# The mixing stage of a two-layer convolution kernel: steps of 8 rows instead of 4, and another split of the nine depthwise taps

## The chip, the cores and the metric

The kernel runs on one core of a Trainium2 chip, in one launch. The metric is the device time of that launch in microseconds (us). The kernel before takes 5684.54 us in the median of three runs (5683.73 to 5684.84). Engines: PE is TensorE (matmuls), PEld its weight loads, DVE VectorE, ACT ScalarE, POOL GpSimd, SP SyncE, which here only issues DMAs.

## The reference

The input `x` is (8, 128, 256, 256) in float32. Two layers follow each other. In short:

```python
# layer 0
h = concat(haar_dwt(group_norm(x)))            # 4*128 channels, 128x128 pixels
h = gelu(batchnorm(conv1x1(h, w_c1, b_c1)))    # 128 channels
res = h
o = dwconv3x3(h, dw_w, dw_b)                   # nine taps per channel, zero padding
o = layernorm_chw(o, gn_g, gn_b)               # mean and variance over one batch element
o = gelu(conv1x1(o, pw1_w, pw1_b))
h = conv1x1(o, pw2_w, pw2_b) + res             # called u in the kernel
h = gelu(batchnorm(conv1x1(h, w_c2, b_c2)))    # 4*128 channels
x = x + haar_idwt(h)
# layer 1
x = x + blur4x4(group_norm(x))
```

## The kernel before, in words

The work is in three stages, one after the other, each a block of instruction streams, one stream an engine. `phase_conv1` (lines 157 to 404) reads `x`, works out its statistics and writes `z`, the output of the first 1x1 convolution without its batch norm, to a scratch in HBM (`z_scratch`), with sums for the batch norm beside it. `phase_mix` (lines 439 to 850) is the mixing stage: batch norm and gelu of `z`, depthwise convolution, layer norm, two pointwise convolutions, residual. It writes `u` to `u_scratch`, and adds up the Gram matrix of `u` (128x128, and the sums as column 129), from which the batch norm of the third stage is worked out. `phase_tail` does the rest. The change touches `phase_mix` alone and the constants ahead of it.

In the mixing stage the 128 channels lie on the partitions. A unit of work is 4 rows of 128 pixels, 512 columns wide, one PSUM bank; a batch element has `STEPS` = 32 units, all eight have `ALL2` = 256. The loops are unrolled in Python: each engine has a loop over a step number `p`, and in each step it does different parts for different units. What a unit `e` goes through:

- SP loads its 4 rows of `z` into `z_in` (L545, four slots).
- ACT does gelu with the batch norm's scale and shift into `h_ring`, called `plane` in the code (L810). It holds 41 blocks of 4 rows with a zero column at each side; between two batch elements lies a block of zero rows, set by POOL (L582). `plane` keeps `h` until the residual reads it.
- The nine taps of the depthwise convolution are split. PE does 2 (`PE_TAPS`) as matmuls with diagonal matrices into `dw_psum`, which has two banks used in turn (L730). DVE does 4 as multiply-adds on `dw_psum`, in place, the fourth into `depthwise_out` (L650); each waits for the one before. ACT does 3 as products with a scale into `tap_products` (L838). POOL adds the three products in two adds (L601) and then adds their sum to `depthwise_out` (L605).
- DVE takes statistics of the finished unit (L657, `bn_stats`).
- After the last unit of a batch element DVE, PE and POOL work out mean and variance over all channels (L665 to L677, L780, L593 with `pow`), and DVE folds the result into the weights and bias of the first pointwise convolution (L682 to L684, L689, with L783 on PE).
- The second half of a unit `l` runs `LEAVE` = 39 steps behind `p`, 35 or 36 behind its depthwise work, since it needs the statistics of its whole batch element: pointwise matmul 1 (L746), gelu (L820), pointwise matmul 2 (L739), residual on DVE (L638), store of `u` (L550), four transposes into `transpose_psum` (L755), copy to SBUF by ACT (L827), four Gram matmuls (L765).

So there are three stretches: 36 steps with depthwise work alone (the filling), 220 with both halves, and 36 to 37 with the second half alone (the draining). The order of the parts inside a step is written out by hand in each engine's loop (L698, L769, L841, L586, L552). Every float32 matmul appears as two records in the trace, and as one half of a `x2` in the rows here.

Of the kernel before, what the change touches and what calls it, by code (L numbers as in the profile page):

```python
# [19 lines left out]
BANK = 512  # L20
# [407 lines left out]
LAG_Z = 1  # L428
LAG_TR = 1
LAG_EVAC = 2  # L430
LAG_GRAM = 3
LAG_DW = 3
LAG_TAPS = 4
LAG_LAST = 3
LAG_STATS = 5
AHEAD = 2


def phase_mix(nc, kp, pw1, pw2, const, z_d, u_d):
# [3 lines left out]
    with ExitStack() as ctx:  # L443
# [3 lines left out]
        plane = sb("h_ring", [128, 4 * BLOCKS + 2, W2 + 2])  # L447
        o_buf = sb("depthwise_out", [128, O_SLOTS, BANK])
        z_in = sb("z_in", [128, 4, BANK])
        diag = sb("tap_diagonals", [128, PE_TAPS, C])  # L450
# [3 lines left out]
        v_t = sb("gelu1_out", [128, 2, BANK])  # L454
        products = sb("tap_products", [128, 2, ACT_TAPS, BANK])
        u_t = sb("u_tile", [128, 4, BANK])
        u_tr = sb("u_transposed", [128, 2, 4, C + 1])
        bst = sb("o_stats", [128, STEPS, BN_W])
# [11 lines left out]
        small = ps("small2", [128, 4])  # L470
# [11 lines left out]
        s_z = [sem(f"z_loaded{i}") for i in range(4)]  # L482
        s_h = sem("h_rows_ready")
        s_dw = sem("dw_psum_ready")
# [15 lines left out]
        s_gm = sem("gram_step_done")  # L500
        s_gacc = sem("gram_added")
        s_ust = [sem(f"u_stored{i}") for i in range(4)]
# [5 lines left out]
        def block_of(e):  # L508

            return e // STEPS * (STEPS + 1) + e % STEPS  # L510

        def tap(k, e):

            kh, kw = k // 3, k % 3
            r = block_of(e) % BLOCKS * R2 + kh
            return plane[:, r:r + R2, kw:kw + W2]

        def rows_of(e):
            r = 1 + block_of(e) % BLOCKS * R2
            return plane[:, r:r + R2, 1:1 + W2]  # L520

        def freed_by(at):

            if at < BLOCKS:
                return None
            b, j = divmod(at - BLOCKS, STEPS + 1)
            return b * STEPS + min(j, STEPS - 1)
# [8 lines left out]

        @block.sync
        def _(sp):
            sp.dma_start(K[:, 0:C], const[:, 0:C]).then_inc(s_id, 16)

            def load(e):
                if e >= 4:
                    sp.wait_ge(s_h, e - 3)
# [948 lines left out]
```

## Time and profile before

| | |
|---|---|
| median of three runs | 5684.54 us |
| the profiled execution's own time | 5687.8 us |
| span of its instructions | 5685.9 us |
| first stage | 0 to about 1237 us |
| mixing stage | about 1237 to 2583 us |
| third stage | about 2583 us to the end |
| busy over the whole span: PE, DVE, ACT, POOL | 92%, 77%, 65%, 36% |
| mean granted clock of TensorE | 0.968 |
| DMA rate in the mixing stage, steps with both halves | 102 to 111 GB/s |

The page of the profile cuts the span into 40 equal slices of 142 us. Of these the mixing stage holds the slices 9 to 18. In them POOL, which does nothing in the first stage, is 7 to 8 tenths busy, DVE 9, ACT 7 to 8, and PE 9, which in the page stands for 90% or more. A busy share says how much of an engine's time is taken and not what holds a step up; for that the rows below come from the timeline.

### The profile page before, as it was taken

What the parts mean: (1) busy time and instruction counts of PE and PEld (TensorE: products, weight loads), DVE (VectorE), ACT (ScalarE), POOL (GpSimd) and SP (SyncE); (2) the same over time, 40 slices, a digit from 0 to 9 for tenths busy, and PEclk for the clock granted to TensorE, in tenths of its full rate; (3) what the DMA queues carried; (4) which work ended last, traced back from release to release, by engine and by line L of the source; (5) the groups of instructions that cost most, each with busy time, mean ns of one, the idle gap of its engine ahead of it and who ended that gap; (6) DMA issues with size and microseconds to landing.
All of it is one profiled execution on the core that took longest, in us unless ns stands there. A gap on an engine that the chain in (4) does not pass through costs nothing. (4 is left out here: it accounts for less than half of the span.)

```text
span 5685.9 us, 67157 instructions
## 1 busy us (share of the span) xinstructions
PE 5206.1 (92%) x18136; PEld 3152.4 (55%) x18136; DVE 4380.2 (77%) x5325; ACT 3721.4 (65%) x5012; POOL 2068.4 (36%) x1397
## 2 busy tenths in 40 slices
PE   2888888986999999996689999999999999999999
PEld 1333333332555555563256666666666766666677
DVE  8555555428999999957988888888888888888833
ACT  0333333346778777754678788787887877878744
POOL 0000000028777777730023333333333333333354
PEclk9999999998999999998899999999999999999999
DMA  9999999842333333326999999999999999999986
GB/s 368 374 372 380 369 380 378 345 143 71 108 108 112 104 108 108 108 83 226 326 381 403 393 401 398 390 402 384 398 392 384 394 384 397 399 384 395 400 292 228
DMA packets 829594, 1729.83 MB, mean 304 GB/s; under 512 B 50064, under 2 KB 587152, under 8 KB 718608
## 3 DMA queue, kind: packets, MB, share of 16 engines
q1 hardware_dynamic: 755472, 1389.81, 66.9%
q10 hardware_dynamic: 73728, 335.58, 14.4%
q8 instruction: 148, 2.42, 0.2%
q14 instruction: 246, 2.02, 0.1%
HBM read 1050.95 MB, written 674.23 MB: 303 GB/s over the span
## 5 line engine op out<-in xcount | busy, mean ns | idle before, releaser
L1080 POOL TENSOR_TENSOR y_lo<-y_centred_tile,y_hi 128x1024 fp32r<-128x1024 f32 x512 | 1042.3, 2057 | 1728.4 <-ACT y_centred_tile L1416 1422.9
L1295 PE MATMUL blur_psum<-y_hi,band_hi 128*128 128x512 f32 x4096 | 1129.3, 417 | 8.9 <-DVE y_tile L1173 7.4
L1278 PE MATMUL conv_psum<-u_in,w_conv 128*128 128x512 f32 x2048 | 975.3, 620 | 106.2 <-DVE pair_sums L1151 81.2
L1295 PE MATMUL blur_psum<-y_lo,band_hi 128*128 128x512 f32 x4096 | 1041.8, 396 | 6.7 <-POOL y_lo L1080 6.3
L1295 PEld LDWEIGHTS blur_psum<-y_hi,band_hi 128*128 128x128 f32 x4096 | 765.8, 188 | 278.8 <-issue 100.6
L1151 DVE TENSOR_TENSOR pair_sums<-gelu_out,conv_psum 128x512 f32<-128x512 f32 x1024 | 653.1, 683 | 308.7 <-ACT conv_psum L1386 308.6
L1295 PEld LDWEIGHTS blur_psum<-y_lo,band_hi 128*128 128x128 f32 x4096 | 769.7, 188 | 199.4 <-POOL y_lo L1080 14.8
L1173 DVE SCALAR_TENSOR_TENSOR y_tile<-blur_psum,rstd_all,y_tile 128x1024 f32<-128x1024 f32 x512 | 639.4, 1276 | 160.5 <-PE blur_psum L1295 153.1
L1386 ACT ACTIVATE gelu_out<-conv_psum,bn_shift,bn_scale 128x512 f32<-128x512 f32 x512 | 397.5, 776 | 534.1 <-PE conv_psum L1278 512.7
L1278 PEld LDWEIGHTS conv_psum<-u_in,w_conv 128*128 128x128 f32 x2048 | 399.4, 198 | 559.7 <-issue 406.2
L601 POOL TENSOR_TENSOR tap_products<-tap_products 128x512 f32<-128x512 f32 x512 | 653.5, 1276 | 42.7 <-ACT tap_products L838 6.2
L838 ACT ACTIVATE tap_products<-h_ring,vectors 128x512 f32<-128x512 f32 x768 | 498.9, 712 | 216.8 <-POOL depthwise_out L605 216.7
L311 DVE BATCH_NORM_STATS2 x_stats<-x_resident 128x6 f32<-128x512 f32 x640 | 395.2, 681 | 293.6 <-DMA x_resident<-x 292.5
L1159 DVE TENSOR_TENSOR quad_sums<-pair_sums 128x1024 f32<-128x1024 f32 x512 | 604.5, 1222 | 8.4
L1166 DVE SCALAR_TENSOR_TENSOR x_tile<-quad_sums,x_tile 128x2048 f32<-128x2048 f32 x256 | 597.0, 2332 | 15.0 <-DVE quad_sums L1159 1.4
L372 PE MATMUL z_psum<-x_resident,w_folded 128*128 128x512 f32 x1280 | 599.4, 624 | 5.2 <-ACT z_psum L397 5.2
L1414 ACT ACTIVATE y_hi<-y_tile,neg_mean_all 128x2048 fp32r<-128x2048 f32 x256 | 513.2, 2004 | 137.9 <-POOL y_lo L1080 133.4
L650 DVE SCALAR_TENSOR_TENSOR dw_psum<-h_ring,vectors,dw_psum 128x512 f32<-128x512 f32 x768 | 578.0, 753 | 25.3 <-PE dw_psum L730 6.8
L393 ACT ACTIVATE z_tile<-z_psum,z_bias 128x512 f32<-128x512 f32 x256 | 175.9, 687 | 643.5 <-DMA z_scratch<-z_tile 438.8
L730 PE MATMUL dw_psum<-h_ring,tap_diagonals 128*128 128x512 f32 x1024 | 504.8, 617 | 62.4 <-DVE depthwise_out L650 52.3
L1397 ACT ACTIVATE junk<-x_tile,neg_group_mean 128x2048 bf16<-128x2048 f32 x256 | 511.6, 1999 | 59.0 <-DVE x_tile L1166 55.9
L1416 ACT ACTIVATE y_centred_tile<-y_tile,neg_mean_all 128x2048 f32<-128x2048 f32 x256 | 509.6, 1991 | 0.0
(168 smaller groups left out, 5445.2 us busy)
## 6 DMA issues: line engine op xcount, KB each, us to landing
x_tile<-x SPq DMA_DIRECT2D x256, 1024.0 KB, 10.1
y_scratch<-x_tile ACTq DMA_DIRECT2D x256, 1024.0 KB, 8.4
y_tile<-y_scratch SPq DMA_DIRECT2D x512, 512.0 KB, 10.9
out<-y_tile SPq DMA_DIRECT2D x512, 512.0 KB, 10.4
x_stream<-x SPq DMA_DIRECT2D x192, 1024.0 KB, 11.6
x_resident<-x SPq DMA_DIRECT2D x160, 1024.0 KB, 11.0
z_scratch<-z_tile ACTq DMA_DIRECT2D x256, 256.0 KB, 7.2
z_in<-z_scratch SPq DMA_DIRECT2D x256, 256.0 KB, 3.6
```

What stands on the lines that cost most here:

```text
L372: ins = nc.tensor.matmul(zp[q % ZP][:, half * BANK:(half + 1) * BANK], w_f[:, p, :], px[:, p // 2, p % 2, rows, :], start=(p == 0), stop=( ...
L601: nc.gpsimd.tensor_tensor(pr[:, 0, :], pr[:, 0, :], pr[:, n, :], ALU.add).then_inc(s_add, 1)
L650: taps.link(nc.vector.scalar_tensor_tensor(to.rearrange("p (r c) -> p r c", c=W2), tap(k, e), V[:, V_DWW + k:V_DWW + k + 1], acc.rearrange ...
L1080: nc.gpsimd.tensor_tensor(y_lo[:, h, part, 2:2 + W], y_c[:, part, :], y_hi[:, h, part, 2:2 + W].bitcast(F32), ALU.subtract).then_inc(s_lo, 1)
L1151: ins = nc.vector.tensor_tensor(sums_t[:, 2 * m + p, :], g_t[:, k % 2, p, :], cv[2 * p + 1][:], op)
L1159: ins = nc.vector.tensor_tensor(dv[:, :, e], sv[:, :, 0], sv[:, :, 1], op)
L1166: nc.vector.scalar_tensor_tensor(x_t[:, i, :], d_t[:], 0.5, x_t[:, i, :], ALU.mult, ALU.add).then_inc(s_y, 1)
L1173: nc.vector.scalar_tensor_tensor(y_t[:, g % YS, t], bl[t][:], rs_b[:, bass.ds(n, 1)], y_t[:, g % YS, t], ALU.mult, ALU.add).then_inc(s_ev, 1)
L1278: nc.tensor.matmul(cv[s][:], w[:, s * C:(s + 1) * C], u_t[:, k % US, :], start=True, stop=True).then_inc(s_mm, 1)
L1295: ins = nc.tensor.matmul(bl[t][:, 2 * c:2 * c + 2, :], wt[:, kw, :], y[:, h, ch:ch + 2, kw:kw + W], start=(m == 0 and kw == 0), stop=(m == ...
L1397: nc.scalar.activation(junk[:], x_t[:, i, :], ACT.Square, bias=neg_gm[:, bass.ds(b, 1)], accum_out=y_sq[:, bass.ds(b, 1), k]).then_inc(s_s ...
L1414: nc.scalar.activation(y_hi[:, h, :, 2:2 + W], src, ACT.Identity, bias=nm_b[:, bass.ds(n, 1)]).then_inc(s_hi, 1)
```

## The change

- A unit is 8 rows, 1024 columns (`R2 = 8`, `UNIT2`). `STEPS` is 16, `ALL2` 128. Instructions of DVE, ACT and POOL on a unit are 1024 wide, matmuls, transposes, copies of transposes and `bn_stats` stay at 512 and come twice (`HALF`, `HALVES`).
- The ring holds 6 blocks of 8 rows instead of 41 of 4. The rows of `h` are therefore stored back to `z_scratch` over their `z` (`store_h`) and loaded again for the residual into `h_in` (`load_h`).
- The split of the taps is 3 on PE, 3 on DVE, 3 on ACT for the first 19 units (`ALONE`), which run with no second half beside them, and 1 on PE, 4 on DVE, 4 on ACT for the other 109. Four products take three adds on POOL, and one more into `depthwise_out`.
- `tap_products` is a ring of six 1024-wide slots. `dw_psum` is one tensor of two banks, used by every unit; in the filling the tensor of pointwise 2 takes every second unit. `transpose_psum` has one bank, used half by half. The small results use banks of others.
- The second half runs `LEAVE` = 21 steps of 8 rows behind `p`.
- The order within a step is another on each engine; DVE puts the statistics of the unit before and the folding between its first and second tap.

```diff
-R2 = BANK // W2
+R2 = 8
+UNIT2 = R2 * W2
+HALF = BANK
 STEPS = H2 // R2
 ALL2 = B * STEPS
-PE_TAPS = 2
-ACT_TAPS = 3
-DVE_TAPS = TAPS - PE_TAPS - ACT_TAPS
...
-BEHIND = 7
-LEAVE = STEPS + BEHIND
-BLOCKS = STEPS + 1 + BEHIND + 1
-O_SLOTS = STEPS + BEHIND - 3
...
+HALVES = 2 * STEPS
+RING = 6
+O_SLOTS = 19
+PR_SLOTS = 6
+LOADED = 3
+
+LEAVE = 21
+ALONE = LEAVE - 2
+LAG_TAPS = 2
+LAG_STATS = 3
+LAG_COLUMNS = LAG_STATS - 1
+LAG_NORM = LAG_COLUMNS + 1
+LAG_BIAS = LAG_NORM + 1
+FIRST_TAPS = (3, 3, 3)
+STEADY_TAPS = (1, 4, 4)
...
+def split_of(e):
+
+    return FIRST_TAPS if e < ALONE else STEADY_TAPS
...
-        dw_p = [ps(f"dw_psum{i}", [128, BANK]) for i in range(2)]
-        p1_p = ps("pw1_psum", [128, BANK])
-        p2_p = ps("pw2_psum", [128, BANK])
-        tr_p = [ps(f"transpose_psum{i}", [128, BANK]) for i in range(2)]
+        dw_p = ps("dw_psum", [128, UNIT2])
+        p1_p = ps("pw1_psum", [128, UNIT2])
+        p2_p = ps("pw2_psum", [128, UNIT2])
+        tr_p = ps("transpose_psum", [128, BANK])
...
+        def tap_psum(e):
+
+            return p2_p if e < ALONE and e % 2 == 1 else dw_p
...
+            def store_h(e):
+                sp.wait_ge(s_h, e + 1)
+                sp.dma_start(by_rows(part(zv, e)), rows_of(e)).then_inc(s_hst[e % 8], 16)
+
+            def load_h(l):
+                if l >= LOADED:
+                    sp.wait_ge(s_u, l - LOADED + 1)
+                sp.wait_ge(s_hst[l % 8], 16 * (l // 8 + 1))
+                sp.dma_start(h_in[:, l % LOADED, :], part(zv, l)).then_inc(s_hin[l % LOADED], 16)
...
+            for p in range(ALL2 + LEAVE + 1):
+                l = p - LEAVE
+                if p + 2 < ALL2:
+                    load_z(p + 2)
+                if 0 <= p - 1 < ALL2:
+                    store_h(p - 1)
+                if 0 <= l + 2 < ALL2:
+                    load_h(l + 2)
+                if 0 <= l - 1:
+                    store_u(l - 1)
...
+            for e in range(ALL2):
                 b, j = divmod(e, STEPS)
                 if j == STEPS - 4:
                     gap(b)
...
+                for n in range(1, split_of(e)[2]):
+                    sum_products(e, n)
+                    if n == 1 and j == 1 and b >= 1:
+                        power(b + 1)
+                pool.wait_ge(s_add, ADD_BEFORE[e + 1])
+                pool.wait_ge(s_lk_tap, DVE_BEFORE[e + 1])
                 o = o_buf[:, e % O_SLOTS, :]
-                nc.gpsimd.tensor_tensor(o, o, pr[:, 0, :], ALU.add).then_inc(s_oo, 1)
+                nc.gpsimd.tensor_tensor(o, o, products[:, ACT_BEFORE[e] % PR_SLOTS, :], ALU.add).then_inc(s_oo, 1)
...
+            for p in range(LAG_TAPS, ALL2 + LEAVE + 2):
+                l, e = p - LEAVE, p - LAG_TAPS
...
+                if j == LAG_BIAS and 1 <= b <= B:
+                    norm_bias(b - 1)
                 if 0 <= l < ALL2:
                     residual(l)
...
+                if j == LAG_NORM and 1 <= b <= B:
                     norm_variance(b - 1)
...
+                if tapping:
+                    add_tap(e, 0)
                 if 0 <= p - LAG_STATS < ALL2:
                     statistics(p - LAG_STATS)
-                if j == LAG_STATS - 1 and 1 <= b <= B:
+                if j == LAG_COLUMNS and 1 <= b <= B:
                     norm_columns(b - 1)
+                if j == LAG_NORM and 1 <= b <= B:
+                    norm_fold(b - 1)
+                if tapping:
+                    for n in range(1, split_of(e)[1]):
+                        add_tap(e, n)
...
+                before = e - 2 if e < ALONE else e - 1
+                if before >= 0:
+                    pe.wait_ge(s_lk_tap, DVE_BEFORE[before + 1])
+                count = split_of(e)[0]
+                for half in range(2):
+                    for k in range(count):
+                        ins = nc.tensor.matmul(tap_psum(e)[:, half * HALF:(half + 1) * HALF], diag[:, k, :],
+                                               tap(k, e, half * R2 // 2, R2 // 2),
+                                               start=(k == 0), stop=(k == count - 1))
+                    ins.then_inc(s_dw, 1)
...
+                if 0 <= l + 1 < ALL2:
+                    pw1_step(l + 1)
+                if 0 <= l - 1 < ALL2:
+                    transpose_half(l - 1, 0)
+                if 0 <= l - 2:
+                    gram_half(l - 2, 1)
...
+                if p - LAG_TAPS < ALL2:
+                    taps_step(p - LAG_TAPS)
+                if 0 <= l - 1 < ALL2:
+                    transpose_half(l - 1, 1)
+                    gram_half(l - 1, 0)
...
+            def tap_product(e, n):
+                if n == 0:
+                    wait_rows(act, e)
+                i = ACT_BEFORE[e] + n
+                if i >= PR_SLOTS:
+
+                    e0, n0 = PRODUCTS[i - PR_SLOTS]
+                    if n0 == 0:
+                        act.wait_ge(s_oo, e0 + 1)
+                    else:
+                        act.wait_ge(s_add, ADD_BEFORE[e0] + n0)
...
+            for p in range(ALL2 + LEAVE + 2):
+                l, e = p - LEAVE, p - LAG_TAPS
+                tapping = 0 <= e < ALL2
+                if p < ALL2:
+                    gelu_first(p)
+                if tapping:
+                    for n in range(2):
+                        tap_product(e, n)
+                if 0 <= l + 1 < ALL2:
+                    gelu_second(l + 1)
+                if 0 <= l - 1 < ALL2:
+                    evacuate(l - 1, 0)
+                if tapping:
+                    for n in range(2, split_of(e)[2]):
+                        tap_product(e, n)
+                if 0 <= l - 1 < ALL2:
+                    evacuate(l - 1, 1)
```

## Rows read from the trace of the kernel before

**Rows 1.** Windows: us, then PE, PEld, DVE, ACT, POOL busy, clock, DMA share, GB/s.

```profile
1250.00:1290.00 40.00, 20.69 (x43) 6.95 (x41) 38.01 (x53) 26.54 (x40) 37.78 (x31) 1.00 0.19 64
1290.00:1380.00 90.00, 53.11 (x87) 17.64 (x88) 80.35 (x115) 59.66 (x90) 83.79 (x68) 0.84 0.21 67
1500.00:1600.00 100.00, 96.79 (x407) 56.53 (x406) 92.46 (x134) 77.71 (x123) 77.08 (x63) 1.00 0.33 106
2484.00:2570.00 86.00, 86.00 (x454) 57.72 (x453) 21.50 (x30) 36.25 (x57) 0.00 (x0) 1.00 0.23 86
```

**Rows 2.** Timeline of PE, one step with both halves: start us, us, then the instruction.

```profile
1746.49 1.02 PE L739 MATMUL pw_psum<-gelu_out,pw_weights 128*128 128x512 f32 x2
...
1748.21 1.88 PE L730 MATMUL dw_psum<-h_ring,tap_diagonals 128*128 128x512 f32 x4
1749.93 0.60 PE L755 MATMUL transpose_psum<-constants,u_tile 128*128 128x128 f32 x4
1751.26 1.02 PE L739 MATMUL pw_psum<-gelu_out,pw_weights 128*128 128x512 f32 x2
```

**Rows 3.** Timeline of the filling: POOL with its first adds, DVE's last tap, PE.

```profile
1243.91 2.68 POOL L601 TENSOR_TENSOR tap_products<-tap_products 128x512 f32<-128x512 f32 x2 [5.74 <-ACT tap_products L838]
...
1253.17 1.27 POOL L605 TENSOR_TENSOR depthwise_out<-depthwise_out,tap_products 128x512 f32<-128x512 f32 x1
1254.39 2.69 POOL L601 TENSOR_TENSOR tap_products<-tap_products 128x512 f32<-128x512 f32 x2
1255.19 0.75 DVE L650 SCALAR_TENSOR_TENSOR depthwise_out<-h_ring,vectors,dw_psum 128x512 f32<-128x512 f32 x1
1256.09 1.10 PE L730 MATMUL dw_psum<-h_ring,tap_diagonals 128*128 128x512 f32 x2 [1.79 <-DVE depthwise_out L650]
1257.16 1.27 POOL L605 TENSOR_TENSOR depthwise_out<-depthwise_out,tap_products 128x512 f32<-128x512 f32 x1
```

**Rows 4.** Groups of POOL: shapes and count, busy us, mean ns, idle before.

```profile
L1080 POOL TENSOR_TENSOR y_lo<-y_centred_tile,y_hi 128x1024 fp32r<-128x1024 f32 x512 | 1042.3, 2057 | 1728.4 <-ACT y_centred_tile L1416 1422.9 <-issue 305.5
L601 POOL TENSOR_TENSOR tap_products<-tap_products 128x512 f32<-128x512 f32 x512 | 653.5, 1276 | 42.7 <-ACT tap_products L838 6.2
L1085 POOL TENSOR_TENSOR seam_lo<-seam_centred_tile,seam_hi 96x256 fp32r<-96x256 f32 x64 | 40.8, 638 | 0.0
```

**Rows 5.** One line of POOL: duration ns as minimum, median, maximum.

```profile
L1080 POOL TENSOR_TENSOR y_lo<-y_centred_tile,y_hi x512: 1990/1999/4052, 2881.7 to 5672.3; 128x1024 fp32r<-128x1024 f32 x171
```

**Rows 6.** Groups of DVE and ACT at 512, 1024 and 2048 columns.

```profile
L1173 DVE SCALAR_TENSOR_TENSOR y_tile<-blur_psum,rstd_all,y_tile 128x1024 f32<-128x1024 f32 x512 | 639.4, 1276 | 160.5 <-PE blur_psum L1295 153.1 <-DVE gn_columns L1222 1.4 <-DVE seam_rstd L1230 1.4
L650 DVE SCALAR_TENSOR_TENSOR dw_psum<-h_ring,vectors,dw_psum 128x512 f32<-128x512 f32 x768 | 578.0, 753 | 25.3 <-PE dw_psum L730 6.8
L657 DVE BATCH_NORM_STATS2 o_stats<-depthwise_out 128x6 f32<-128x512 f32 x256 | 177.7, 694 | 14.9 <-POOL depthwise_out L605 7.1
L1416 ACT ACTIVATE y_centred_tile<-y_tile,neg_mean_all 128x2048 f32<-128x2048 f32 x256 | 509.6, 1991 | 0.0
L838 ACT ACTIVATE tap_products<-h_ring,vectors 128x512 f32<-128x512 f32 x768 | 498.9, 712 | 216.8 <-POOL depthwise_out L605 216.7
```

**Rows 7.** Timeline at the change of the batch element: POOL's power, DVE's folding.

```profile
1850.15 0.55 POOL L593 TENSOR_TENSOR small_columns<-small_columns,neg_half 128x1 f32<-128x1 f32 x1 [2.06 <-DVE small_columns L676]
1853.33 0.16 DVE L682 TENSOR_TENSOR small_columns<-small_columns,vectors 128x1 f32<-128x1 f32 x1
1855.86 0.68 DVE L657 BATCH_NORM_STATS2 o_stats<-depthwise_out 128x6 f32<-128x512 f32 x1
```

**Rows 8.** Timeline: POOL's last add of the stage, and the last Gram sum on DVE.

```profile
2473.68 1.27 POOL L605 TENSOR_TENSOR depthwise_out<-depthwise_out,tap_products 128x512 f32<-128x512 f32 x1 [0.85 <-DVE depthwise_out L650]
2582.59 0.29 DVE L694 TENSOR_TENSOR gram<-gram,gram_psum 128x129 f32<-128x129 f32 x1 [3.82 <-PE gram_psum L765]
```

**Rows 9.** DMA of the whole kernel: packets by size; one issue with its median us to landing.

```profile
DMA packets 829594, 1729.83 MB, mean 304 GB/s; under 512 B 50064, under 2 KB 587152, under 8 KB 718608
...
u_scratch<-u_tile SPq DMA_DIRECT2D x256, 256.0 KB, 2.3
```

More of the change, by code:

```diff
@@ L552, in _, with load_z @@
-            for p in range(-AHEAD, ALL2 + LEAVE):
-                if p + AHEAD < ALL2:
-                    load(p + AHEAD)
-                if p == 0:
-                    sp.dma_start(w1[:], pw1).then_inc(s_w, 16)
-                    sp.dma_start(w2[:], pw2).then_inc(s_w, 16)
-                    sp.dma_start(K[:, C:], const[:, C:]).then_inc(s_w, 16)
-                if p >= LEAVE:
-                    store(p - LEAVE)
+                return d[b, :, j * UNIT2:(j + 1) * UNIT2]
+            def load_z(e):
+                if e >= LOADED:
+                    sp.wait_ge(s_h, e - LOADED + 1)
+                sp.dma_start(z_in[:, e % LOADED, :], part(zv, e)).then_inc(s_z[e % LOADED], 16)
@@ L575, in gap, with power, sum_products @@
                 at = b * (STEPS + 1) + STEPS
[L576 to L586 removed]
+                wait_place(pool, at)
+                r = 1 + at % RING * R2
+                if at % RING == 0:
+                    pool.memset(ring[:, R2 * RING + 1, :], 0.0)
+                if at % RING == RING - 1:
+                    pool.memset(ring[:, 0, :], 0.0)
+                pool.memset(ring[:, r:r + R2:R2 - 1, :], 0.0).then_inc(s_fill, 1)
+            def power(n):
+                pool.wait_ge(s_pow, n)
+                nc.gpsimd.tensor_tensor(t[:, 3:4], t[:, 2:3], neg_half[:, 0:1], ALU.pow).then_inc(s_rs, 1)
+            def sum_products(e, n):
+                first = products[:, ACT_BEFORE[e] % PR_SLOTS, :]
+                pool.wait_ge(s_pr, ACT_BEFORE[e] + n + 1)
+                if n > 1:
+                    pool.wait_ge(s_add, ADD_BEFORE[e] + n - 1)
+                nc.gpsimd.tensor_tensor(first, first, products[:, (ACT_BEFORE[e] + n) % PR_SLOTS, :],
+                                        ALU.add).then_inc(s_add, 1)
+            power(1)
+            for e in range(ALL2):
                 b, j = divmod(e, STEPS)
@@ L626, in _ @@
             dve.wait_ge(s_id, 16)
-            for k in range(PE_TAPS):
+            for k in range(PE_MOST):
                 nc.vector.tensor_scalar(diag[:, k, :], K[:, K_ID:K_ID + C], V[:, V_DWW + k:V_DWW + k + 1],
@@ L643, in depthwise @@
[L643 to L653 removed]
+                dve.wait_ge(s_hin[slot], 16 * (l // LOADED + 1))
@@ L738, in pw2_step @@
                     pe.wait_ge(s_u, l)
-                nc.tensor.matmul(p2_p[:], w2[:], v_t[:, l % 2, :], start=True, stop=True).then_inc(s_p2, 1)
+                else:
+                    pe.wait_ge(s_lk_tap, DVE_BEFORE[ALONE])
+                for half in range(2):
+                    at = slice(half * HALF, (half + 1) * HALF)
+                    ins = nc.tensor.matmul(p2_p[:, at], w2[:], v_t[:, l % 2, at], start=True, stop=True)
+                ins.then_inc(s_p2, 1)
             def pw1_step(l):
@@ L745, in pw1_step @@
                     pe.wait_ge(s_ln, l // STEPS + 1)
-                nc.tensor.matmul(p1_p[:], w1f[:, l // STEPS % 2, :], o_buf[:, l % O_SLOTS, :],
-                                 start=True, stop=True).then_inc(s_p1, 1)
-            def transpose_step(l):
+                for half in range(2):
+                    at = slice(half * HALF, (half + 1) * HALF)
+                    ins = nc.tensor.matmul(p1_p[:, at], w1f[:, l // STEPS % 2, :], o_buf[:, l % O_SLOTS, at],
+                                           start=True, stop=True)
```

299 lines of the change are left out of this document (133 added, 166 removed).

## The prediction

> **What bounds the kernel now.** The change is inside the mixing stage, so I read that stage alone and ask in each of its stretches which engine never waits. The first view is the busy time by stretch [rows 1]. With both halves (1500 to 1600 us) PE is busy 96.79 of 100 us at the full clock, DVE 92.46, ACT 77.71, POOL 77.08. In the filling (1250 to 1290) POOL is busy 37.78 of 40 us and PE only 20.69. In the draining PE is busy all of 86 us. Busy shares don't prove a bound, so the second view is the timeline. With both halves PE starts pointwise 2 at 1746.49 and again at 1751.26, and between them everything follows without a gap: two pointwise matmuls take 1.72 us, two taps 1.72, transposes and Gram 1.33 [rows 2]. A step is 4.77 us and is PE's own work; 8 rows cost 9.54. In the filling POOL starts its last add at 1253.17 and at 1257.16, with its two other adds directly between: 3.99 us a step, POOL's own work, 7.98 for 8 rows [rows 3].
>
> **What the change does to each engine,** per 8 rows with both halves. PE loses two of four tap matmuls: 9.54 - 1.72 = 7.82 us. DVE is busy 92.46/20.96 = 4.41 us a step, 8.82 for 8 rows, with four taps. An operation of its kind with one PSUM operand takes 753 ns at 512 columns and 1276 at 1024 [rows 6], so four taps and one residual 1024 wide are 6.38, and two statistics of 694 make 1.39: 7.77 us. ACT has 7.41 us for 8 rows. Its slope is (1991 - 712)/1536 = 0.83 ns a column, which gives a product 1.14 us at 1024 [rows 6]: four of these replace six of 0.71 (+0.29), and the two gelus save a fixed 0.28 each (712 ns less 512 columns): some 7.1 us. So three engines come below 8 us. What decides is the fourth.
>
> **POOL** gets more work: three adds for four products and one into the output, all 1024 wide. This is the cost to get right. Before it shows an add of this form only at 512: 1276 ns [rows 4]. Its 1024-wide relation is the subtraction in the third stage, 1999 ns in the median [rows 5]; the cheap end is therefore 2.00 us. The dear end is two adds of 512 with nothing saved, 2.55. Between them: two subtractions of one kind, 638 ns at 256 columns and 1999 at 1024, give a fixed part of 0.18 us and 1.77 ns a column. The add doesn't lie on that line (it would be 1.09 us), so its cost for a column is higher; with the same fixed part it is (1.276 - 0.184)/512 = 2.13 ns, and a 1024-wide add takes 2.37 us. The stage's very first pair of adds, with DVE's taps not yet begun, took 2.68 us for two [rows 3], so the higher price is not contention and won't go away. I take 2.37, since it comes from the same instruction.
>
> A rule of the Trainium skill bears on this, GPSIMD Engine Reference, section Performance versus the Vector engine: a two-input add of 2048 float32 columns takes 4497 ns there, because both operands pass one read port. On a line with the 1276 of this trace that makes 2.35 us at 1024, and the sum below would be about 10 us lower. No row here shows a 2048-wide add.
>
> Between dependent adds there is a gap: from the first of two to the last add is 1257.16 - 1254.39 = 2.77 us for two, 1.385 each, 0.11 over the duration; from the last add to the next first it is 1.22, 0.05 under [rows 3]. A step of 8 rows on POOL is 3 x 2.48 + 2.32 = **9.76 us**, more than the 9.54 of PE today. In the filling, with two sums, it is 2 x 2.48 + 2.32 = 7.28 against 7.98.
>
> **Waits that the new order adds.** `dw_psum` is single, so PE's taps wait for DVE's last tap of the unit before, and DVE's first tap waits for PE. That circle is 0.15 us from DVE's last tap to PE (1255.19 + 0.75 to 1256.09 [rows 3]), 1.9 for two matmuls with their tail, 4 x 1.30 for the taps and 1.39 for the statistics between them: 8.65 us. It lies under 9.76, with the residual (1.28) beside PE's matmuls. Behind the waiting PE are half of the transposes and the Gram matmuls, and behind them ACT's second copy; PE has 1.9 us of slack a step, so they catch up. ACT's third product waits for POOL's last add of the unit before; POOL's first sum (2.3 us) covers the 2.2 us of products three and four. The statistics wait for POOL's last add on DVE, with two taps and more behind them; DVE has 2.0 us of slack.
>
> **DMA.** Storing and reloading `h` doubles the traffic: the share of 0.33 at 106 GB/s [rows 1] becomes about 0.66 if a byte costs what it costs now. The store has packets of 512 bytes (a row of 128 pixels). Most packets of the kernel, 587152 of 829594, are under 2 KB, and the kernel still averages 304 GB/s [rows 9]. If the packets of this store alone cost double, the share is 0.8. SP issues four DMAs a step instead of four in two steps; each needed load is issued two steps ahead, 19 us, against 2.3 us to landing for a store of half that size [rows 9]. So I cost this at nothing; POOL's slower step is its cover, and it fails if a store costs four times as much (share over 1).
>
> **The sum,** against the profiled execution (5687.8 us, 3.3 above the median). POOL's first add is at 1243.91 [rows 3]; three gelus and two products are now 0.43 us longer each and the `z` loads twice as large: 4.4 us later, 1248.3. Filling: 19 x 7.28 = 138.3, to 1386.6. There the first folding comes between DVE's first and second tap: POOL's power costs 0.55 [rows 7], and POOL's last add waits for the folding (1853.33 to 1855.86, 2.5 us [rows 7]) and the taps behind it; with the gap rows and the change of split 4.3 us: 1390.9. Then 109 x 9.76 = 1063.8, to 2454.7. The folding in the long stretch: after POOL's first sum (2.3) power 0.55, folding 2.5, three taps 3.9: the last add starts 9.3 us into the step instead of 7.4, plus a memset of 0.3: 2.3 a batch element, seven times 16: 2470.8. POOL's last add ended before at 2473.68 + 1.27 = 2475.0 [rows 8]: 4 us earlier. The draining is PE's own work before, 2582.9 - 2475.0 = 107.9 [rows 8], 3.05 us a step. After, 17 to 18 units are left at 3.44 + 2.66 = 6.10 and 2.5 us for the end: 111.5, 3.5 more, since the second half runs 168 rows behind instead of 156. Together -0.5 us: 5687 for the profiled execution, **5684 us** for the median. So the matmul time saved turns up on POOL.
>
> **Rivals.** A measurement of this kernel can tell about 0.2% (11 us) from no change.
> (1) POOL's add is as cheap as the subtraction. For it: the only 1024-wide row of POOL [rows 5]. Against: the add's price at 512 [rows 4]. A step would be 3 x 2.11 + 1.95 = 8.28, so the circle of DVE and PE bounds, 8.65: -1.11 x 109 = -121, and -1.11 x 19 = -21 in the filling: 5542. With a price of 2.2 it is 5684 - 493 x 0.17 = 5600 (4 adds in 109 steps, 3 in 19: 493 us for each us of price). Chance 0.30.
> (2) Slower: no fixed part is saved at 1024 and the add costs 2.55. For it: nothing in a row separates a fixed part from the slope of this add. Against: every other instruction here has one. It decides from 2.39 on, where the sum is over 11 us up; at 2.55 it gives 5684 + 493 x 0.18 = 5773. Chance 0.12.
> (3) Slower: the clock. PE's granted clock was 1.00 in the first part of the filling with PE half idle, but 0.84 later [rows 1]; its two levels are 2.4 and 1.2 GHz. PE will now idle 1.9 of 9.8 us a step. At a mean of 0.84 its 7.82 us become 9.3, still under POOL's 9.76; it decides below 0.80, and at 0.75 a step is 10.4: +70, 5754. Chance 0.06. The Trainium skill, TensorE: Matmul & The Clock Gate, section The HAM clock gate, says that activity releases the throttle; the trace agrees in that the steps with a busy PE have 1.00 [rows 1]. By that rule alone a less busy PE could spend whole steps at the lower level.
> The forecast itself (price 2.3 to 2.4, POOL the bound, waits up to 40 us more or 25 less) has 0.52.
>
> **The numbers.** Of the forecast's 0.52 some 0.11 is faster by over 0.2%, 0.25 within, 0.16 slower. With (1) all faster and (2), (3) slower: faster 0.41, same 0.25, slower 0.34. The range goes from 5550 (nearly all of rival 1) to 5740 (the lower half of 2 and 3); its own without rivals would be 5660 to 5725.
>
> **What would show it.** POOL 1024-wide adds at 2.3 to 2.4 us, POOL busy over 95% in the steps with both halves, a step of 9.8 us, PE busy about 80% and waiting on DVE ahead of its taps; ACT waiting on POOL ahead of its third product; filling steps of 7.3 us; DMA share near 0.66 and no wait on a DMA. A POOL add near 2.0 us, or POOL waiting on DVE or ACT in each step, would show the forecast wrong.

## The result, and the profile after

The changed kernel takes 5733.59 us (median of 4 runs, 5731.33 to 5734.81); before it was 5684.14 in the same comparison (5682.59 to 5684.84). The ratio is 1.0087, with a 95% interval of 1.0069 to 1.0104: slower by 49 us. The forecast had been 5684, with 5660 to 5725 as its own range. The profiled execution took 5734.81 us, for a forecast of 5687.

Windows of the changed kernel, with the columns of [rows 1]: filling, both halves, draining.

```profile
1280.00:1380.00 100.00, 70.50 (x151) 28.92 (x152) 70.70 (x73) 58.70 (x57) 94.12 (x42) 0.92 0.53 151
1580.00:1680.00 100.00, 85.61 (x376) 49.60 (x375) 77.50 (x71) 75.16 (x84) 96.29 (x43) 1.00 0.71 216
2540.00:2600.00 60.00, 55.94 (x288) 37.19 (x287) 11.29 (x10) 19.79 (x27) 0.00 (x0) 1.00 0.51 158
```

With both halves, away from a change of the batch element, POOL is now the engine that never rests (96.29 of 100 us), PE fell from 96.79 to 85.61, and its clock stayed at 1.00. DMA doubled, and between 1420 and 2519 us no engine waits for a transfer. Next the groups of POOL in this stage, which answer to [rows 4, 5].

```profile
L642 POOL TENSOR_TENSOR tap_products<-tap_products 128x1024 f32<-128x1024 f32 x365 | 864.2, 2368 | 45.9 <-ACT tap_products L927 13.0
L657 POOL TENSOR_TENSOR depthwise_out<-depthwise_out,tap_products 128x1024 f32<-128x1024 f32 x128 | 301.2, 2353 | 65.0 <-DVE depthwise_out L705 56.9
```

The price was forecast at 2.37 us and is 2.368. Now POOL's timeline: one step of the filling, then one with both halves, each from last add to last add.

```profile
1302.71 2.35 POOL L657 TENSOR_TENSOR depthwise_out<-depthwise_out,tap_products 128x1024 f32<-128x1024 f32 x1
1305.02 4.88 POOL L642 TENSOR_TENSOR tap_products<-tap_products 128x1024 f32<-128x1024 f32 x2
1309.97 2.35 POOL L657 TENSOR_TENSOR depthwise_out<-depthwise_out,tap_products 128x1024 f32<-128x1024 f32 x1
...
2100.24 2.36 POOL L657 TENSOR_TENSOR depthwise_out<-depthwise_out,tap_products 128x1024 f32<-128x1024 f32 x1
2102.55 7.40 POOL L642 TENSOR_TENSOR tap_products<-tap_products 128x1024 f32<-128x1024 f32 x3
2110.02 2.35 POOL L657 TENSOR_TENSOR depthwise_out<-depthwise_out,tap_products 128x1024 f32<-128x1024 f32 x1
```

A regular step is 9.78 us (forecast 9.76), a filling step 7.26 (7.28), with no idle time between the adds. So the regular steps are as forecast, and the 48 us by which the profiled execution missed its forecast are elsewhere. Three rows locate them: POOL's last add of the 19th unit, of the last unit, and the last Gram sum of the stage.

```profile
1402.18 2.34 POOL L657 TENSOR_TENSOR depthwise_out<-depthwise_out,tap_products 128x1024 f32<-128x1024 f32 x1 [4.64 <-DVE depthwise_out L705]
...
2516.98 2.34 POOL L657 TENSOR_TENSOR depthwise_out<-depthwise_out,tap_products 128x1024 f32<-128x1024 f32 x1
...
2640.30 0.29 DVE L751 TENSOR_TENSOR gram<-gram,gram_psum 128x129 f32<-128x129 f32 x1 [5.22 <-PE gram_psum L842]
```

The 19th unit ended at 1404.5 (forecast 1390.9: +13.6), the 109 steps after it took 1114.8 (forecast 1079.9: +34.9), the draining from 2519.3 to 2640.6 took 121.3 (forecast 111.5: +9.8). Together the stage ends 58.3 us later than forecast; the rest of the kernel took 10.7 less than in the profiled execution of before.

The largest part is at the change of the batch element. Of the timeline there, POOL and DVE:

```profile
1862.61 7.36 POOL L642 TENSOR_TENSOR tap_products<-tap_products 128x1024 f32<-128x1024 f32 x3
...
1865.14 2.36 DVE L721 TENSOR_TENSOR small_columns<-o_mean_var,vectors 128x1 f32<-128x1 f32 x1
...
1872.02 2.35 POOL L657 TENSOR_TENSOR depthwise_out<-depthwise_out,tap_products 128x1024 f32<-128x1024 f32 x1 [2.05 <-DVE depthwise_out L705]
...
1873.33 1.06 DVE L732 TENSOR_TENSOR small_columns<-vectors,small_columns 128x1 f32<-128x1 f32 x1
...
1878.12 1.43 DVE L739 TENSOR_TENSOR small_columns<-small_columns,vectors 128x1 f32<-128x1 f32 x1
...
1879.91 2.18 DVE L741 SCALAR_TENSOR_TENSOR small_columns<-small_columns,vectors 128x1 f32<-128x1 f32 x1
...
1886.08 2.36 POOL L657 TENSOR_TENSOR depthwise_out<-depthwise_out,tap_products 128x1024 f32<-128x1024 f32 x1 [4.01 <-DVE depthwise_out L705]
```

Operations on one column (128x1) take up to 2.36 us here. L732 ends at 1874.39; POOL's add that began at 1872.02 ends at 1874.37. L721 ends at 1867.50, where the second of POOL's three sums ends (1862.61 plus two thirds of 7.36 is 1867.52). DVE's taps queue behind them, and POOL's last add waits for the taps: 2.05 and 4.01 us idle. That was the theory to test: **a small operation of DVE that reads two operands in SBUF waits until POOL's running add is over.** The mean durations of two such operations in the stage (eight of each), first in the changed kernel, then the same two before (L684 is L741 there, L666 is L721):

```profile
L721 DVE TENSOR_TENSOR small_columns<-o_mean_var,vectors 128x1 f32<-128x1 f32 x8 | 14.5, 1814 | 0.3
L741 DVE SCALAR_TENSOR_TENSOR small_columns<-small_columns,vectors 128x1 f32<-128x1 f32 x8 | 13.5, 1692 | 0.3
```

```profile
L684 DVE SCALAR_TENSOR_TENSOR small_columns<-small_columns,vectors 128x1 f32<-128x1 f32 x8 | 8.1, 1013 | 0.3
L666 DVE TENSOR_TENSOR small_columns<-o_mean_var,vectors 128x1 f32<-128x1 f32 x8 | 1.9, 236 | 0.3
```

Before, POOL's adds were 1.27 us long and left gaps, so a wait was at most about that. The Trainium skill, SBUF — State Buffer, section Who interferes with whom, says that a DVE instruction with two inputs in SBUF contends with a GpSimd instruction that reads SBUF, and that the port pair which they share is an exclusive lock. The trace agrees: L732 lasts until the running add ends, to within 0.02 us.

A second thing happens at the same places. Windows of 30 us at a change of the element, two of the changed kernel and one of before:

```profile
1704.00:1734.00 30.00, 21.09 (x80) 11.89 (x80) 26.40 (x28) 18.31 (x20) 23.29 (x12) 0.89 0.61 175
1867.00:1897.00 30.00, 21.71 (x74) 12.80 (x74) 24.19 (x27) 18.16 (x20) 22.16 (x11) 0.77 0.56 157
```

```profile
1685.00:1715.00 30.00, 26.79 (x112) 15.34 (x111) 27.97 (x46) 20.29 (x33) 21.11 (x18) 1.00 0.28 90
```

PE first stands idle (2.6 to 3.1 us ahead of the averaging matmul), and then its granted clock falls to 0.50, the lower of its levels, for some microseconds: in all six changes of the long stretch in the changed kernel, in two of six before. Four of its tap matmuls, 1.88 us at the full clock, take 3.11 to 3.75. So the clock is a rival to the waits of DVE, and the experiments have to part the two.

### The profile page after: what moved, and what is told of

Read it like the earlier page. It is cut to its first block and busy times, and to the rows that moved or that the text cites. A ratio compares the mean times of both kernels' runs of the same rounds, so it can differ in the third digit from the quotient of the medians.

```text
span 5733.0 us, 64191 instructions
## 1 busy us (share of the span) xinstructions
PE 5110.5 (89%) x17776; PEld 3092.9 (54%) x17776; DVE 4241.7 (74%) x4667; ACT 3680.4 (64%) x4512; POOL 2255.4 (39%) x1123
## 3 DMA queue, kind: packets, MB, share of 16 engines
q10 hardware_dynamic: 73728, 335.58, 14.2%
q14 instruction: 230, 1.88, 0.1%
## 5 line engine op out<-in xcount | busy, mean ns | idle before, releaser
L642 POOL TENSOR_TENSOR tap_products<-tap_products 128x1024 f32<-128x1024 f32 x365 | 864.2, 2368 | 45.9 <-ACT tap_products L927 13.0
L927 ACT ACTIVATE tap_products<-h_ring,vectors 128x1024 f32<-128x1024 f32 x493 | 537.2, 1139 | 292.7 <-POOL depthwise_out L657 292.7
L705 DVE SCALAR_TENSOR_TENSOR dw_psum<-h_ring,vectors,dw_psum 128x1024 f32<-128x1024 f32 x347 | 445.6, 1284 | 128.5 <-PE dw_psum L793 124.3
L372 PE MATMUL z_psum<-x_stream,w_folded 128*128 128x512 f32 x768 | 400.0, 676 | 114.2 <-DMA x_stream<-x 114.2
## 6 DMA issues: line engine op xcount, KB each, us to landing
x_resident<-x SPq DMA_DIRECT2D x160, 1024.0 KB, 11.2
```

Of the source, the lines that this page charges most:

```text
L372: ins = nc.tensor.matmul(zp[q % ZP][:, half * BANK:(half + 1) * BANK], w_f[:, p, :], px[:, p // 2, p % 2, rows, :], start=(p == 0), stop=( ...
L642: nc.gpsimd.tensor_tensor(first, first, products[:, (ACT_BEFORE[e] + n) % PR_SLOTS, :], ALU.add).then_inc(s_add, 1)
L927: nc.scalar.activation(by_rows(products[:, i % PR_SLOTS, :]), tap(k, e), ACT.Copy, scale=V[:, V_DWW + k:V_DWW + k + 1]).then_inc(s_pr, 1)
```

## The experiments

Every kernel was timed beside the kernel before on the same chip, and ratios are to that (5686.21 us in the median of 18 runs for the first four, 5685.46 of 7 for the rest). Differences in us to the changed kernel are to its 5733.59 of the comparison above. The theories under letters are told in the expectations themselves.

**The small operations in another form, alone.** The changed kernel, with five of the small layer-norm operations written as tensor_scalar, whose second operand is a pointer to a column of scalars instead of a tensor:

```diff
-ln.link(nc.vector.tensor_tensor(t[:, 0:1], mv[:, 0:1], V[:, V_DWB:V_DWB + 1], ALU.add))
+ln.link(nc.vector.tensor_scalar(t[:, 0:1], mv[:, 0:1], V[:, V_DWB:V_DWB + 1], None, ALU.add))
...
-nc.vector.scalar_tensor_tensor(t[:, 7:8], t[:, 8:9], t[:, 6:7], V[:, V_GNB:V_GNB + 1],
-                               ALU.mult, ALU.add).then_inc(s_ln, 1)
+nc.vector.tensor_scalar(t[:, 7:8], t[:, 8:9], t[:, 6:7], V[:, V_GNB:V_GNB + 1],
+                        ALU.mult, ALU.add).then_inc(s_ln, 1)
```

> The changed kernel with five small DVE operations of the layer norm in another form: tensor_scalar with column pointers instead of tensor_tensor or scalar_tensor_tensor with two operands in SBUF. Theory A (a small DVE operation with two SBUF operands waits until the POOL add in progress ends; now the adds are 2.37 us long and follow each other without a pause): the four that took 2.36, 1.06, 1.43 and 2.18 us take 0.15 to 0.25, the two long steps per batch element (11.45 and 14.05 us) become about 9.8 and 12, and the time falls from 5734 by 25 us or so, to 5700 to 5715. Theory B (the loss at the change of a batch element comes from the order: PE's averaging matmul behind a gelu, the folding ahead of three taps, TensorE's clock): the operations may get shorter, but the wait appears elsewhere and the time stays within 5 us of 5734.

Measured: 5707.04 us (5 runs, 5701.88 to 5718.3), ratio 1.0036 (1.0022 to 1.0049), 27 us below the changed kernel. Groups of DVE in the stage:

```profile
L740 DVE TENSOR_SCALAR pw_folded<-pw_weights,small_columns 128x128 f32<-128x128 f32 x8 | 11.9, 1492 | 0.3
...
L741 DVE TENSOR_SCALAR small_columns<-small_columns,vectors 128x1 f32<-128x1 f32 x8 | 2.2, 273 | 0.3
```

The five fell to 203 to 273 ns. POOL's last adds at a change of the element are now mostly 9.77 and 11.89 us apart, for 11.45 and 14.05: 3.8 us less. One wait was left over and grew: the folding of the weights, L740 (128x128 from SBUF to SBUF), had been sheltered behind the others (287 ns) and now meets a running add itself (1492 ns). In its timeline it runs from 1871.27 to 1873.39, again to within 0.1 us of the end of an add of POOL.

```profile
1870.94 4.87 POOL L642 TENSOR_TENSOR tap_products<-tap_products 128x1024 f32<-128x1024 f32 x2
...
1871.27 2.12 DVE L740 TENSOR_SCALAR pw_folded<-pw_weights,small_columns 128x128 f32<-128x128 f32 x1
1873.42 0.27 DVE L741 TENSOR_SCALAR small_columns<-small_columns,vectors 128x1 f32<-128x1 f32 x1
```

By these traces the lower clock doesn't make this gain. It still fell once at each change, and at two of the six this slowed the four tap matmuls behind the averaging one (3.59 and 2.89 us; 1.96 at the other four): the two steps there are 9.77 and 11.89 us in any case. It shows one step later, where two of the six changes have 11.9 us instead of 10.1 (the two with the longest stretch at the lower clock), as two of the changed kernel's do (12.0 and 12.1). That is some 2 us at each of these two, in both kernels. At the first folding, in the filling, the forms won only 1.8 us.

**The same forms in the kernel before** (the same five lines in before's code).

> The kernel before with the same five operations in the form with one SBUF operand. Theory A: before the change only one of them waited for a POOL add (the last of the folding, 1.12 us instead of 0.22), and the stall of a batch element is about 4 us, of which at most 1 goes: 5684 falls by 3 to 8 us. Theory B: no change, 5684 within 2 us.

Measured: 5678.84 us (12 runs), ratio 0.9985 (0.9976 to 0.9993): 7 us gained, a quarter of what the same edit gives after the change. So the cost came mostly with the change: POOL's adds became longer and lost their pauses, and no run parts these two. Of the 27 us, 7 had been there before, and some 20 are new.

**The statistics behind the taps, alone.** In DVE's program the calls of statistics and of the norm's columns move behind the four taps of the step:

```diff
                 if tapping:
                     add_tap(e, 0)
-                if 0 <= p - LAG_STATS < ALL2:
-                    statistics(p - LAG_STATS)
-                if j == LAG_COLUMNS and 1 <= b <= B:
-                    norm_columns(b - 1)
...
                         add_tap(e, n)
+                if 0 <= p - LAG_STATS < ALL2:
+                    statistics(p - LAG_STATS)
+                if j == LAG_COLUMNS and 1 <= b <= B:
+                    norm_columns(b - 1)
```

> The changed kernel with DVE's statistics (and the columns worked out from them) behind the last tap of a step instead of between the first and the second tap. Theory A (POOL's four adds bound a step): the step stays 9.77 us, DVE's waits only move, and the time stays within 10 us of 5734. Theory C (the circle of PE's tap matmuls and DVE's taps, 8.65 us with the statistics in it, holds the step, and POOL only follows): the step falls by up to the 1.3 us of the statistics, 109 times, to about 5600 to 5650.

Measured: 5727.62 us (4 runs), ratio 1.0076 (1.006 to 1.0092). The regular step stays at 9.78: taking 1.39 us out of the circle between DVE and PE does nothing, so that circle doesn't bound the changed kernel. At a change of the element the first of the two long steps goes (9.77), the 14.04 stays, and the step after it is 11.8 to 13.0 us at four of six, where the changed kernel has 12.0 and 12.1 at two and 10.1 at the rest; hence only 6 us.

**More taps on PE.** Split 2 PE, 4 DVE, 3 ACT in the steps with both halves, which takes one sum from POOL:

```diff
-STEADY_TAPS = (1, 4, 4)
+STEADY_TAPS = (2, 4, 3)
```

> The changed kernel with 2 taps on PE, 4 on DVE and 3 on ACT in the steps with both halves too. POOL has then 7.27 us of adds a step and PE 9.54. Theory A with the circle as I have it (0.15 + 3.6 for four matmuls + 5.2 for four taps + 1.35 for statistics = 10.3 us): a step of 10.3 to 10.4 us bound by PE and DVE waiting for each other, and 5734 + 109 x 0.6 = about 5795. Theory D (engines overlap well enough and only the busiest counts): a step of 9.54 us, PE bound as before the change, about 5705.

Measured: 5785.21 us (4 runs), ratio 1.0177 (1.0162 to 1.0193). POOL's timeline:

```profile
2102.86 2.37 POOL L657 TENSOR_TENSOR depthwise_out<-depthwise_out,tap_products 128x1024 f32<-128x1024 f32 x1 [3.17 <-DVE depthwise_out L705]
...
2113.16 2.36 POOL L657 TENSOR_TENSOR depthwise_out<-depthwise_out,tap_products 128x1024 f32<-128x1024 f32 x1 [3.10 <-DVE depthwise_out L705]
```

A step is 10.30 us and POOL waits 3.1 of it: with one sum less POOL no longer bounds, and what does is the circle. It had been forecast at 8.65 for one PE tap; another (four matmuls, 1.72 us) makes 10.37. So the circle's size follows too, 0.07 under its forecast; that it is the circle and not PE's order is what the next run shows.

**Both together:** split 2, 4, 3 and the statistics behind the taps.

> The split 2, 4, 3 of the run before, with the statistics behind the taps. Theory A: the statistics leave the circle of PE's tap matmuls and DVE's taps, which shrinks from the 10.30 us measured to about 0.15 + 3.6 + 5.2 = 9.0, and POOL needs 7.27; PE's own work of 9.54 us then bounds, so the steps become 9.55 us and the time about 5705. Rival E (the step of 10.30 us was not the circle but PE's order, with ACT's copies between its transposes): the step stays near 10.3 us and the time near 5785.

Measured: 5737.24 us (4 runs, 5726.19 to 5745.61), ratio 1.0084 (1.0063 to 1.0105), between the two expectations. The trace says why. The regular step did fall to 9.53:

```profile
2103.36 2.37 POOL L657 TENSOR_TENSOR depthwise_out<-depthwise_out,tap_products 128x1024 f32<-128x1024 f32 x1 [2.35 <-DVE depthwise_out L705]
...
2112.90 2.37 POOL L657 TENSOR_TENSOR depthwise_out<-depthwise_out,tap_products 128x1024 f32<-128x1024 f32 x1 [2.33 <-DVE depthwise_out L705]
```

The window with both halves, columns as above:

```profile
1580.00:1680.00 100.00, 100.00 (x421) 58.72 (x420) 80.77 (x75) 70.08 (x79) 73.15 (x33) 1.00 0.78 223
```

PE is busy 100 of 100 us: this is the kernel before's bound in steps of 8 rows (9.54). But the change of the element costs more, 16.4 to 18.1 us and 11.8 or 13.5 for two steps of 9.53. The columns of the norm come later in DVE's queue, PE stands idle 4.06 us for them, and then does its taps at the lower clock. PE and DVE at one change:

```profile
1704.18 6.74 PE L793 MATMUL dw_psum<-h_ring,tap_diagonals 128*128 128x512 f32 x8
...
1711.03 1.29 DVE L705 SCALAR_TENSOR_TENSOR dw_psum<-h_ring,vectors,dw_psum 128x1024 f32<-128x1024 f32 x1 [5.58 <-PE dw_psum L793]
```

In a regular step these eight take 3.60 us. At the six changes they took 6.21, 6.74, 5.38, 5.38, 5.38 and 5.07, and the long step was 17.5, 18.05, 16.5, 16.5, 16.5 and 16.4, in the same order: with no slack left, the lower clock is paid nearly in full, 2.3 us a change in that step alone. In all, 0.25 us gained in each of 107 steps (27 us) stands against 3.6 more lost at each of six changes (22); the expectation left the second term out. In its trace the steps from the first unit to the last took 10 us less than in the changed kernel, and the draining 2 more. That the time was no better came from the rest of the kernel, 16 us longer in this execution, of which more below.

**Alternating splits.** POOL bounds with (1, 4, 4), PE with (2, 4, 3) and the late statistics. So even units take the first and odd ones the second, with the late statistics and the forms of the first experiment:

```diff
+OTHER_TAPS = (2, 4, 3)
...
-    return FIRST_TAPS if e < ALONE else STEADY_TAPS
+    if e < ALONE:
+        return FIRST_TAPS
+    return STEADY_TAPS if e % 2 == 0 else OTHER_TAPS
```

> The changed kernel with the statistics behind the taps, the small operations in the form with one SBUF operand, and the two splits in turn: 1, 4, 4 on even units and 2, 4, 3 on odd ones. Theory A (each engine's own work bounds): POOL has 9.77 and 7.27, mean 8.52 us; PE 7.82 and 9.54, mean 8.68; DVE 7.8. Two steps take about 17.4 us instead of 19.56, and the time is 5707 - 54 x 2.2 = about 5590. Rival F (POOL and PE are heavy in different units and the single dw_psum and six product slots don't let one run ahead): each pair costs the larger of both each time, 9.77 + 9.54, and the time stays above 5690.

Measured: 5617.89 us (4 runs, 5613.59 to 5629.01), ratio **0.9875** (0.9859 to 0.9892): faster than both kernels. POOL's timeline of a step with three sums:

```profile
2104.09 2.38 POOL L660 TENSOR_TENSOR depthwise_out<-depthwise_out,tap_products 128x1024 f32<-128x1024 f32 x1
...
2113.89 2.35 POOL L660 TENSOR_TENSOR depthwise_out<-depthwise_out,tap_products 128x1024 f32<-128x1024 f32 x1
```

The window with both halves:

```profile
1580.00:1680.00 100.00, 97.81 (x428) 58.78 (x428) 86.78 (x88) 77.86 (x89) 95.64 (x43) 1.00 0.81 242
```

Steps alternate between 9.80 and 7.55 us: 17.35 a pair for 19.56, 2.2 less in some 53 pairs, 118 us, where 116 were gained over the changed kernel. So the gain is that of the pairs. The stall at a change is no smaller than in the changed kernel (7.4 to 8.1 us for 6.9), although the forms of the first experiment are in it. PE (97.81) and POOL (95.64) are now both nearly full. It stays 28 us above the expectation, which had the pair right and not the steps around a change of the element (11.9, 11.6 and 9.5 us, where the pattern would give 7.55, 9.8 and 7.55). The alternation wasn't tried without the other two edits.

**The same, with split 3 PE, 4 DVE, 2 ACT in the filling**, where PE idles. (ACT also waits for the first depthwise outputs before it refills the ring's first row.)

```diff
-FIRST_TAPS = (3, 3, 3)
+FIRST_TAPS = (3, 4, 2)
```

> The run with alternating splits, and in the first 19 units 3 taps on PE, 4 on DVE, 2 on ACT instead of 3, 3, 3. Theory A: in the filling POOL has two adds a unit (4.8 us), PE 5.2, DVE 4 x 1.30 + 1.35 = 6.6: the filling step falls from 7.27 to about 6.6 us, and the time by some 12 us against the alternating run. If the filling is held by something else (the loads of z, TensorE at its lower clock), the step stays near 7.3.

Measured: 5614.36 us (4 runs, 5605.88 to 5618.01), ratio 0.9874 (0.9857 to 0.989): not told apart from the run before it; the expectation was some 12 us less. POOL's timeline in the filling shows that the step did shorten, to 6.48 us, and that POOL now waits for DVE's last tap in each:

```profile
1298.79 2.35 POOL L660 TENSOR_TENSOR depthwise_out<-depthwise_out,tap_products 128x1024 f32<-128x1024 f32 x1 [1.79 <-DVE depthwise_out L708]
...
1305.27 2.35 POOL L660 TENSOR_TENSOR depthwise_out<-depthwise_out,tap_products 128x1024 f32<-128x1024 f32 x1 [1.80 <-DVE depthwise_out L708]
```

The sixteen steps up to the first folding take 14 us less, and the three of the folding 5.5 more (17.6, 8.9 and 15.5 us for 11.0, 10.6 and 15.0): part of the gain ends in a wait that is there anyway, and the 8.6 us left are of the size by which the runs of one kernel differ here (5605.88 to 5618.01).

**The disputed cost by itself.** The changed kernel, with one more operation of DVE on one column in each step, behind the statistics; its output is not used. Even units take the form with two tensors, odd ones the form with a pointer:

```diff
+to = probe_out[:, e:e + 1]
+if e % 2 == 0:
+    nc.vector.tensor_tensor(to, V[:, 0:1], V[:, 1:2], ALU.add)
+else:
+    nc.vector.tensor_scalar(to, V[:, 0:1], V[:, 1:2], None, ALU.add)
```

> The changed kernel with one small DVE operation more in each step, behind the statistics: on even units a tensor_tensor of one column with both operands in SBUF, on odd units a tensor_scalar of the same column with the second operand as a column pointer. Its result is not used. Theory A: the tensor_scalar takes about 0.2 us each time. The tensor_tensor starts some 1.3 us into POOL's first add of the step and ends when that add ends, so it takes about 1.1 us each time; DVE has 2 us of slack, so steps and time stay (5734). Theory B (the long small operations at the change of a batch element were waits for something else, such as the semaphore of the operation before): both take 0.16 to 0.2 us.

Durations of the two forms (minimum, median, maximum):

```profile
L778 DVE TENSOR_TENSOR probe_out<-vectors x64: 142/1039/2330, 1257.3 to 2524.2; 128x1 f32<-128x1 f32 x64
L780 DVE TENSOR_SCALAR probe_out<-vectors x64: 194/197/205, 1263.7 to 2533.7; 128x1 f32<-128x1 f32 x64
```

One case of each in the timeline, with POOL:

```profile
2101.96 0.20 DVE L780 TENSOR_SCALAR probe_out<-vectors 128x1 f32<-128x1 f32 x1
...
2110.39 7.39 POOL L643 TENSOR_TENSOR tap_products<-tap_products 128x1024 f32<-128x1024 f32 x3
...
2111.74 1.04 DVE L778 TENSOR_TENSOR probe_out<-vectors 128x1 f32<-128x1 f32 x1
```

The same sum of the same two columns takes 197 ns in one form, whatever POOL does, and anything from 142 ns to 2.33 us in the other. At 2111.74 it ends at 2112.78; the first of POOL's three sums ends 2.37 us after 2110.39, at 2112.76. That shows the wait and which form has it. The time, 5760.06 us (2 runs), ratio 1.0128 (1.0108 to 1.0148), missed the expectation, which had no cost: regular steps kept 9.78 us, but at a change of the element the steps became 13.7, 14.2 and 11.2 us for 11.45, 14.05 and 10.1. There the added operation stands ahead of the late taps: 3.5 us a change, 21 for six, of 26 measured. A wait of DVE is free in a regular step and is paid there.

## Why the prediction was wrong

**Right, with their numbers.** The bound went from PE to POOL. POOL's add was 2.368 us for 2.37 forecast; the line to the Trainium skill's figure (GPSIMD Engine Reference, Performance versus the Vector engine) gave 2.35, so the measurement lies nearer to the fixed part taken from the trace. Step 9.78 for 9.76, filling step 7.26 for 7.28, circle 8.6 for 8.65 (from the split 2, 4, 3), PE busy 85.61% for about 80, DMA share 0.71 for 0.66 without a wait. Rival 1 (cheap add) and rival 2 (2.55) fall with the price; rival 3, a lower clock through whole steps, falls with 1.00 in the window with both halves. At the changes of the element the clock did fall, which no term of the sum held. In all regular steps the change costs nearly nothing, as the sum said.

**Wrong: the stall at the change of the batch element.** The step of the sum was "2.3 a batch element, seven times 16". It holds the folding at 2.5 us, the length that it has beside POOL's adds of 1.27 [rows 7], and left the columns of the norm out, for which DVE had "2.0 us of slack". But most of these 2.5 us was itself waiting for POOL, as the two operations behind the L682 of [rows 7] show (before):

```profile
1853.52 1.26 DVE L683 TENSOR_SCALAR pw_folded<-pw_weights,small_columns 128x128 f32<-128x128 f32 x1
1854.82 1.12 DVE L684 SCALAR_TENSOR_TENSOR small_columns<-small_columns,vectors 128x1 f32<-128x1 f32 x1
```

With POOL at rest they take 0.29 and 0.22. In the row of the changed kernel the folding takes 4.0 us, from 1878.12 to 1882.09. (The seven was one too many as well: of the eight elements one is folded in the filling and one behind the last tap, so six changes lie in the long stretch.) Measured are 44.4 us in the 107 steps behind the first folding: six changes of 6.9 us each (four of 6.2, two of 8.4) and a memset of 0.37 for each of seven elements. With the forms experiment four are 2.4 and two 4.2, so 3.8 to 4.2 us less, like for like; forecast were 2.0 without the memset. The 2 us more at two changes, in either kernel, go with the longer stretch at the lower clock. The forms won 27 of the 49 us, of which the same edit won 7 before the change as well. So the term had its place right and its size wrong, and the cause is that longer adds of POOL lengthen every small two-tensor operation of DVE. The rows that showed it were in the trace of before and were not read.

**Wrong: the first folding and the start,** 13.6 us. "With the gap rows and the change of split 4.3 us" was taken. The first add came 3.5 us later than forecast, and the first unit's last add 2.4 later than two sums behind it. These 5.9 us are no shown miss: in the six other traces with the same filling the stage's first add lies anywhere from 1244.1 to 1256.5, around the 1248.3 forecast. The rest is at the first folding:

```profile
1375.86 0.59 PE L870 MATMUL pw_psum<-small_columns,mean_over_channels 128*128 128x2 f32 x2 [10.22 <-DVE small_columns L722]
...
1376.31 8.05 PE L793 MATMUL pw_psum<-h_ring,tap_diagonals 128*128 128x512 f32 x12
...
1390.37 2.34 POOL L657 TENSOR_TENSOR depthwise_out<-depthwise_out,tap_products 128x1024 f32<-128x1024 f32 x1 [4.42 <-DVE depthwise_out L705]
```

PE waited 10.22 us for the columns with the next taps behind it, and then did twelve tap matmuls in 8.05 us, at a granted clock of 0.50 (eleven had taken 4.88 at 1360.76). POOL's adds of the following units waited 2.93, 4.42 and 4.64 us for DVE. That is 8 us more than forecast, and 4 more in the next two steps. The small operations' form explains little of it (1.8 us in the forms experiment); what is left is PE's place in its own queue and its lower clock, and no run parts these two.

**Wrong: the draining,** "17 to 18 units are left at 3.44 + 2.66 = 6.10". A unit takes 6.74. The timeline of one:

```profile
2534.21 0.60 PE L831 MATMUL transpose_psum<-constants,u_tile 128*128 128x128 f32 x4
...
2536.16 0.63 PE L831 MATMUL transpose_psum<-constants,u_tile 128*128 128x128 f32 x4 [0.45 <-ACT u_transposed L912]
...
2540.95 0.60 PE L831 MATMUL transpose_psum<-constants,u_tile 128*128 128x128 f32 x4
```

There is one bank of PSUM for transposes. With 8 rows a unit has two sets of transposes close behind each other, and the second waits until ACT has copied the first. In steps of 4 rows there were two banks, and the pointwise matmuls stood between the sets. 0.64 us in each of 17 to 18 units covers the 9.8 us. This is read from the trace; a run with a second bank wasn't made.

**The rest of the kernel** was 10.7 us shorter than in the profiled execution of before, which hid a fifth of the loss. It isn't an effect of the change: in the profiled executions of these ten kernels, whose code behind the mixing stage is the same, it takes 3094 to 3097 us in six and 3105 to 3111 in four, the kernel before among the four, and kernels with the changed stage in both groups. What sets it wasn't tried.

## What to carry to other kernels

When operations of POOL get longer, price not only POOL: look through DVE's stream for small instructions with two operands in SBUF, and see whether their durations vary with nothing to do with their size; where they stand ahead of late work, write them with a pointer operand, or put them where POOL rests. If an engine's bound moves by a split of work, the best split need not be a whole number in each step: alternating two splits filled both engines (0.9875), where either alone lost. And work out the steps around a rare event (here every 16th) by their own timeline, with the lower clock that an idle PE comes back to; most of this loss was there, some in the draining, and none in the regular steps.

## What the runs showed of the hardware

- An operation on 128x1 that reads two tensors in SBUF took 142 ns to 2.33 us beside POOL's 1024-wide adds, and where it waited it ended within 0.02 us of the end of an add; as tensor_scalar with a pointer it took 194 to 205 ns. The trace shows the wait as duration, not as idle time.
- A tensor_scalar of 128x128 from SBUF to SBUF waits as well (287 ns with POOL at rest or behind another wait, 1492 in the mean and 2.12 us in the row above), while the same form on 128x1 doesn't.
- POOL's two-input add took 1276 ns at 512 columns and 2368 at 1024; the line through them has a fixed part of 0.18 us.
- At each change of the element, after PE had stood idle (2.6 to 3.1 us in the changed kernel, 4.06 with the split 2, 4, 3 and late statistics), its granted clock fell to 0.50 and its matmuls took about twice as long: eight of 512 columns up to 6.74 us for 3.60. In the kernel before, where PE waited 0.48 us ahead of the averaging matmul and 2.73 for the folding, it fell at two of six changes.
